# A four-layer hybrid network on one core: split down product with streamed weights, and a rearranged attention opening

## The reference, cut to what matters

```python
x = x + attn_a(layernorm(x))   # 16 heads of 16, rope, causal, LoRA on q, k, v, o
x = x + ffn(layernorm(x))      # 4 experts, the best one for each row
x = x + mamba(layernorm(x))    # chunked scan, gate, norm
x = x + ffn(layernorm(x))      # the same weights again

# ffn
probs = softmax(x @ Wr + br);  top_w, top_idx = top_k(probs, 1)
h = silu(x @ Wg[e]) * (x @ Wu[e])          # 256 -> 1024
y = (h @ Wd[e]) * top_w                    # 1024 -> 256, e = top_idx
```

## Time and profile before

| | us |
|---|---|
| median of 3 runs | 2194.78 |
| lowest and highest | 2182.81, 2199.73 |
| the profiled execution's own time | 2185.0 |
| its span, first to last instruction | 2183.1 |

### The profile page before, as it was taken

The page is one execution under the profiler, slowest core; times in us unless marked ns, Lnnn a source line. Parts: engine busy times, 40 slices in busy tenths (PEclk is TensorE's granted clock), DMA queues, the critical chain, the costliest instruction groups (busy, mean ns, idle before and its releaser), DMA issues. The chain is left out here.

```text
span 2183.1 us, 30159 instructions
## 1 busy us (share of the span) xinstructions
PE 1819.3 (83%) x9520; PEld 1212.1 (56%) x9520; DVE 1191.3 (55%) x2979; ACT 822.7 (38%) x1705; POOL 725.6 (33%) x922
## 2 busy tenths in 40 slices
PE   5368889889888864899999658989898938999997
PEld 3133334434433322788888535747484727888886
DVE  4466676666666508543443356665656685443442
ACT  2036655656665624111111035554646441111111
POOL 2335464464462312222222124333242312222221
PEclk9569989989988855999999969999999978999999
DMA  5522333332442108000000230100101080000000
GB/s 160 174 89 90 119 126 95 122 125 77 134 135 87 39 16 313 22 24 28 26 25 26 70 111 15 43 36 1 78 1 78 1 309 22 26 24 30 25 24 9
DMA packets 90179, 161.23 MB, mean 74 GB/s; under 512 B 23080, under 2 KB 50476, under 8 KB 88880
## 3 DMA queue, kind: packets, MB, share of 16 engines
q1 hardware_dynamic: 71504, 107.39, 14.7%
q0 software_dynamic: 17984, 50.62, 7.2%
q10 hardware_dynamic: 544, 1.31, 0.2%
HBM read 102.52 MB, written 45.48 MB: 68 GB/s over the span
## 5 line engine op out<-in xcount | busy, mean ns | idle before, releaser
L690 ACT ACTIVATE a_probs<-a_ps_e 128x512 f32<-128x512 f32 (+3 forms) x768 | 336.0, 491 | 204.1 <-PE a_ps_e L854 200.9
L438 DVE CUSTOM_DVE_ANT_0 a_ps_m<-a_ps_m,a_causal 128x512 f32<-128x512 f32 (+3 forms) x512 | 239.4, 517 | 97.5 <-PE a_ps_m L841 96.4
L1433 PE MATMUL g_ps_y<-g_w_d,x_res 128*128 x1120 | 253.2, 379 | 2.8 <-DVE x_res L1203 2.8
L854 PE MATMUL a_ps_e<-a_q_st,a_k_st 64*128 64x512 f32 (+3 forms) x768 | 187.9, 480 | 76.4 <-ACT a_probs L690 48.5
L854 PEld LDWEIGHTS a_ps_e<-a_q_st,a_k_st 64*128 64x128 f32 x768 | 79.6, 201 | 289.8 <-ACT a_probs L690 200.5
L1433 PEld LDWEIGHTS g_ps_y<-g_w_d,x_res 128*128 128x128 f32 x1120 | 212.3, 190 | 34.6 <-issue 3.2
L442 DVE TENSOR_REDUCE a_peak<-a_ps_m 128x1 f32<-128x512 f32 x256 | 164.8, 686 | 94.8 <-PE a_ps_m L841 94.1
L841 PE MATMUL a_ps_m<-a_k_st,a_q_st 64*128 64x512 f32 (+3 forms) x768 | 152.7, 399 | 68.8 <-DMA a_k_st<-a_scr_k 28.0
L1323 ACT COPY x_res<-g_ps_h 128x512 f32<-128x512 f32 x70 | 41.1, 587 | 439.2 <-PE g_ps_h L1441 439.2
L576 POOL TENSOR_SCALAR_AFFINE_SELECT a_probs<-a_probs 128x256 f32<-128x256 f32 x256 | 103.9, 408 | 284.1 <-ACT a_probs L690 283.8
L1170 DVE BATCH_NORM_STATS2 g_xe_stats<-x_res 128x6 f32<-128x256 f32 x70 | 29.9, 426 | 295.6 <-DMA x_res<-g_x_rows,g_token_i 295.6
(11 more groups left out here) (272 smaller groups left out, 3664.5 us busy)
## 6 DMA issues: line engine op xcount, KB each, us to landing
a_q_st<-a_scr_q POOLq DMA_DIRECT2D x32, 512.0 KB, 4.0
a_k_st<-a_scr_k POOLq DMA_DIRECT2D x32, 512.0 KB, 4.8
m_spread_acs<-m_acs_rows SPq DMA_DIRECT2D x8, 2048.0 KB, 9.7
a_scr_q<-a_high SPq DMA_DIRECT2D x36, 256.0 KB
a_scr_k<-a_high SPq DMA_DIRECT2D x36, 256.0 KB
a_swapped<-a_raw SPq DMA_DIRECT2D x64, 128.0 KB, 2.0
g_w_gu<-L_ffn_Wg SPq DMA_DIRECT2D x8, 1024.0 KB, 9.8
g_w_gu<-L_ffn_Wu SPq DMA_DIRECT2D x8, 1024.0 KB, 12.4
```

The costliest lines, as they stand in the source:

```text
L438: nc.vector.tensor_tensor_reduce(ps_m[:, bank, 0:w], ps_m[:, bank, 0:w], causal[:, 512 - w:], 1.0, MASKED, ALU.add, ALU.max, peak[:, p % 2 ...
L690: nc.scalar.activation(probs[:, N % RING, r, q0:], ps_e[:, (2 * N + r) % HEAD_BANKS, q0:], ACT.Exp, scale=DH ** -0.5).then_inc(exp_done, 1)
L854: nc.tensor.matmul(ps_e[:, (2 * N + r) % HEAD_BANKS, q0:], k_st[rows(r), p % BUFS, j * P:(j + 1) * P], q_st[rows(r), p % BUFS, 512 * c + q ...
L1433: last = nc.tensor.matmul(ps_y[:, 0:D], hid_t[:, f * P:(f + 1) * P], w_d[:, bass.ds(e, 1), f].rearrange("p a d -> p (a d)"), start=(f == 0 ...
```

## The change

Expert layers: `Wd` isn't kept in SBUF. During the last attention units it is split once into a high and a low float32r part and written to a DRAM tensor `down_rows` (`load_down` on SP, `round_down` on ACT, `lower_down` on POOL, `store_down` on SP). For each slot POOL gathers the 128 rows of its expert, 16 KB each, into one of two buffers (`stream`), by a row index that DVE makes from the owner of the slot. The hidden rows are split too: ACT copies both halves to `hid_hi`, DVE subtracts for `hid_lo`. The down product has 8 float32r products of 512 columns (high by high and low side by side) and 8 of 256 (low by high); the result takes two operations. On DVE `center` now comes first in a turn and `stats` last, on POOL `root` last.

Attention: q and k pieces stand at steps 2, 8, 14, 20, and so do the v pieces; swaps, rotations, roundings, remainders and keeps are moved to match, the last of them into the next unit (`ROPE_THEN`). Parts 2 and 3 of block 0 have buffers of their own for high and low (`parts`); ACT issues the keeps of its parts 1 and 3. `put_rows` goes from POOL to SP, and the rows are rounded by ACT's copy. The loads of x for batches 1 to 3 wait for the first pair of heads. The moments of batch 1 stand between maxima, those of batches 2 and 3 in units 1 and 5. The diff, cut to its core:

```diff
-    LORA_AT, XT_AT, OUT_AT, QK_AT, V_AT, LORA_O_AT = (1, 4, 9), (6, 7, 12, 13), (15, 17, 19, 21), (3, 5, 7, 9), (3, 5, 7, 9), 13
+    LORA_AT, XT_AT, OUT_AT, QK_AT, V_AT, LORA_O_AT = (1, 4, 9), (6, 7, 12, 13), (15, 17, 19, 21), (2, 8, 14, 20), (2, 8, 14, 20), 11
...
+        first_high = spare[:, 2560:3584].rearrange("p (n q) -> p n q", n=2)
+        first_low = spare[:, 3584:4608].rearrange("p (n q) -> p n q", n=2)
...
+        wd_raw = [w[:].rearrange("p i q -> p (i q)") for w in (raw, rope)]
+        wd_high = [[x_t[:, 0], x_t[:, 1]], [xn[:].rearrange("p t d -> p (t d)"), swapped[:].rearrange("p i q -> p (i q)")]]
+        wd_rows = C["wd_rows"].rearrange("(e p) (t a d) -> e p t a d", p=P, t=FF // P, a=2)
+        WD_AT = {12 * CORE + 10 + 14 * e: e for e in range(EXPERTS)}
...
+        def parts(blk, i):
+            if blk == 0 and i >= 2:
+                return first_high[:, i % 2], first_low[:, i % 2]
+            return high[:, i % 2], low[:, i % 2]
+
+        def keep(eng, blk, i):
+            eng.wait_ge(low_ready, 4 * blk + i + 1)
+            n, half = i % 2, i // 2
+            to = scr[n][blk % 2, :, :, :, half * 512:(half + 1) * 512]
+            hi, lo = parts(blk, i)
+            for c, part in enumerate(((hi, hi, None, lo), (hi, lo, None, hi))[n]):
+                if part is not None:
+                    eng.dma_start(to[:, c], part).then_inc(scr_out[i % 2], 16)
...
+            def put_rows(p):
+
+                sp.wait_ge(piece_act, ACT_NO["max", p] + 1)
+                for r in range(2):
+                    sp.dma_start(q_st[64 * r + 32:64 * r + 33, p % BUFS, :].bitcast(F32), less_t[r * T:(r + 1) * T, p % 2, :]).then_inc(rows_in[p % BUFS], 16)
...
+            def load_down(e):
+                sp.wait_ge(low_ready, 4 * 2 * BATCH)
+                if e >= 2:
+                    sp.wait_ge(wd_out, 48 * (e - 1))
+                sp.dma_start(wd_raw[e % 2].rearrange("p (t d) -> p t d", d=D), A["Wd"][e].rearrange("(t p) d -> p t d", p=P)
+                             ).then_inc(wd_in, 16)
+
+            def store_down(e):
+                sp.wait_ge(wd_less, 4 * (e + 1))
+                sp.dma_start(wd_rows[e, :, :, 1], wd_raw[e % 2].rearrange("p (t d) -> p t d", d=D)).then_inc(wd_out, 16)
+                for k in range(2):
+                    sp.dma_start(wd_rows[e, :, 4 * k:4 * k + 4, 0], wd_high[e % 2][k].rearrange("p (t d) -> p t d", d=D)
+                                 ).then_inc(wd_out, 16)
...
             for i in range(4):
                 swap(0, i)
-            for i in range(4):
-                keep(0, i)
+            for i in (0, 2):
+                keep(sp, 0, i)
+            sp.wait_ge(pair_in[0], 32)
             for b in range(1, BATCH):
                 sp.dma_start(X[:, b * T:(b + 1) * T], x[:, b * T:(b + 1) * T]).then_inc(x_in[b], 16)
-            for i in range(4):
+            for i in range(3):
                 swap(1, i)
-            for i in range(4):
-                keep(1, i)
+            keep(sp, 1, 0)
+            put_rows(0)
+            swap(1, 3)
+            for i in (1, 2):
+                keep(sp, 1, i)
+            put_rows(1)
+            keep(sp, 1, 3)
...
                 for n in range(CORE):
+                    for p in MAX_AT.get(U * CORE + n, []):
+                        put_rows(p)
...
-                    if g % 2 == 1 and more and n in (4, 6, 8, 11):
-                        swap(2 * b + 2 + g // 2, (4, 6, 8, 11).index(n))
-                    if g % 2 == 1 and more and n in (17, 19):
-                        keep(2 * b + 2 + g // 2, (17, 19).index(n))
-                    if g % 2 == 0 and U >= 2 and (U - 1) // GROUPS + 1 < BATCH and n in (3, 6):
-                        keep((U - 1) // GROUPS * 2 + 2 + (U - 1) % GROUPS // 2, 2 + (3, 6).index(n))
+                    if g % 2 == 1 and more and n in (3, 9, 15, 21):
+                        swap(2 * b + 2 + g // 2, (3, 9, 15, 21).index(n))
+                    if g % 2 == 1 and more and n in (14, 20):
+                        keep(sp, 2 * b + 2 + g // 2, (14, 20).index(n))
+                    if g % 2 == 0 and U >= 2 and (U - 1) // GROUPS + 1 < BATCH and n in (3, 9):
+                        keep(sp, (U - 1) // GROUPS * 2 + 2 + (U - 1) % GROUPS // 2, 2 + (3, 9).index(n))
                     if n == (22 if g == 0 else 11):
                         collect(U, 0)
+                    if U * CORE + n in WD_AT:
+                        load_down(WD_AT[U * CORE + n])
+                    if U * CORE + n - 21 in WD_AT:
+                        store_down(WD_AT[U * CORE + n - 21])
...
-            for b in range(1, BATCH):
-                dve.wait_ge(x_in[b], 16)
-                moments(b)
-            maxima(0, CUTS[0])
+            for k in range(0, CUTS[0], 2):
+                maxima(k, k + 2)
+                if k in range(22, 22 + 2 * T, 2):
+                    row_moments(1, (k - 22) // 2)
+                if k == 42:
+                    moments(1)
...
+                    if g == 1 and b + 2 < BATCH and n in range(10, 10 + T):
+                        row_moments(b + 2, n - 10)
+                    if g == 1 and b + 2 < BATCH and n == 20:
+                        moments(b + 2)
...
+            def lower_down(e, k):
+                pool.wait_ge(wd_rounded, 4 * e + k + 1)
+                part = wd_raw[e % 2][:, 512 * k:512 * k + 512]
+                high_part = wd_high[e % 2][k // 2][:, 512 * (k % 2):512 * (k % 2) + 512]
+                nc.gpsimd.tensor_tensor(part.bitcast(F32R), part, high_part, ALU.subtract).then_inc(wd_less, 1)
...
                 if i >= 1:
                     remainder(1, i - 1)
-                if i == 2:
-                    put_rows(0)
+            inverse_std(1)
             remainder(1, 3)
-            put_rows(1)
-
-            ROPE_AT = {6: (0, 0), 7: (0, 1), 8: (0, 2), 9: (1, 0), 10: (1, 1), 11: (1, 2), 12: (2, 0), 13: (2, 1),
-                       14: (2, 2), 15: (0, 3), 17: (1, 3), 19: (3, 0), 21: (3, 1), 23: (3, 2)}
+
+            ROPE_AT = {5: (0, 0), 6: (0, 1), 7: (0, 2), 11: (1, 0), 12: (0, 3), 13: (1, 1), 14: (1, 2), 17: (2, 0),
+                       18: (1, 3), 19: (2, 1), 20: (2, 2), 23: (3, 0)}
+            ROPE_THEN = {0: (3, 1), 1: (2, 3), 2: (3, 2), 7: (3, 3)}
...
+                    if g % 2 == 0 and U >= 2 and (U - 1) // GROUPS + 1 < BATCH and n in ROPE_THEN:
+                        blk, (i, part) = (U - 1) // GROUPS * 2 + 2 + (U - 1) % GROUPS // 2, ROPE_THEN[n]
+                        if part < 3:
+                            rotate(blk, i, part)
+                        else:
+                            remainder(blk, i)
+                    for k in range(4):
+                        if U * CORE + n - 11 - 2 * k in WD_AT:
+                            lower_down(WD_AT[U * CORE + n - 11 - 2 * k], k)
...
-                    for p in MAX_AT.get(U * CORE + n - 1, []):
-                        put_rows(p)
+                    if g == 1 and b + 2 < BATCH and n == 22:
+                        inverse_std(b + 2)
...
-                    nc.scalar.copy(less_t[:, k % 2], bank[0:2 * T, 0:P]).then_inc(piece_act, 1)
+                    nc.scalar.copy(less_t[:, k % 2].bitcast(F32R), bank[0:2 * T, 0:P]).then_inc(piece_act, 1)
...
-                if blk >= 1 or i >= 2:
+                if blk >= 1:
                     act.wait_ge(scr_out[i % 2], 48 * (2 * blk + i // 2))
-                nc.scalar.copy(high[:, i % 2].bitcast(F32R), raw[:, i]).then_inc(high_ready, 1)
+                nc.scalar.copy(parts(blk, i)[0].bitcast(F32R), raw[:, i]).then_inc(high_ready, 1)
...
                     for i in range(4):
                         round_high(0, i)
+                    for i in (1, 3):
+                        keep(act, 0, i)
                 if e in ACT_NO:
...
-                    if g % 2 == 1 and more and n in (11, 14, 21):
-                        round_high(2 * b + 2 + g // 2, (11, 14, 21).index(n))
-                    if g % 2 == 0 and U >= 2 and (U - 1) // GROUPS + 1 < BATCH and n == 2:
+                    if g % 2 == 1 and more and n in (10, 16, 23):
+                        round_high(2 * b + 2 + g // 2, (10, 16, 23).index(n))
+                    if g % 2 == 0 and U >= 2 and (U - 1) // GROUPS + 1 < BATCH and n == 5:
                         round_high((U - 1) // GROUPS * 2 + 2 + (U - 1) % GROUPS // 2, 3)
...
-        w_d = sb("w_d", [P, EXPERTS, FT, D])
+        with nc.sbuf_tensor(name + "later", [P, 4608 + P], F32) as held_later:
+            later = held_later[:]
+        w_d = sb("w_d", [P, 2, FT, 2 * D], F32R)
...
-        hid_t = flat[:, 0:FF]
-        rows = flat[:, FF:FF + 2 * D].rearrange("p (a d) -> p a d", a=2)
+        hid_hi, hid_lo = C["hid"]
+        row_index = sb("row_index", [P, SLOTS], U32)
+        rows = flat[:, 2 * FF:2 * FF + 2 * D].rearrange("p (a d) -> p a d", a=2)
...
-            sp.wait_ge(turned_ps, HALVES)
-            for e in range(EXPERTS):
```

(64 more changed lines are left out.)

54 lines of the change are left out of this document (28 added, 26 removed).

## The result

The changed kernel takes 2263.4 us in the median of four runs (2260.2 to 2265.8), the kernel before 2192.1 in the four runs beside it (2182.8 to 2199.7): a ratio of 1.032 (95% interval 1.028 to 1.036). It is slower by 71 us where I forecast +3. The profiled execution has a span of 2258.5 us for 2183.1.

The account below looks back on a forecast made before the run. PE bounds the expert slots, while attention shows waits on exponentials, the k tile and rows of maxima. Attention -33 and expert layers +36 sum to +3 on 2194.8, giving 2198 us; range 2120 to 2265, the forecast's own 2180 to 2218.

Parts of the forecast that it names:

- the expert slots: Both expert layers: a slot goes from 10.11 to 10.65 us, +35 us over some 66 slots (+3 to +115).
- The loop: Expert slots: result, send, fetch, stream, root, center, combine, hidden transposes close once a slot, about 9.55 us + S.
- S: Expert slots: POOL's issue of the stream gather with 16 KB rows, taken as 1.1 us (0.6 to 2.3).
- Rival A: Expert slots: the loop over POOL doesn't bind, PE alone sets 9.56 us a slot; 2127 us in all; chance 0.22.
- Rival B: Expert slots: S is 2 us or more, 66 us per us; 2258; against it, 0.60 for 4 KB rows; chance 0.23.
- only stalls between them can go, and PE's shown waits in the units are short: -3 (0 to -10): Attention units: spreading the same projections can only remove stalls, -3 us (0 to -10).
- the opening: Start of attention: first scores at 65.5 to 66, maxima no longer only at 88.45; -23 us (-10 to -26).
- The step by which the last writes are issued until about 54 and the loads go at about 59.6: Opening: own buffers and ACT's queue end write issue at about 54, not 60.74; loads follow 5.6 us later.
- rival C: Opening: writes on two queues land no sooner, x comes late, DVE waits for it amid maxima; +20, 2218; chance 0.11.
- the rows of maxima, -11, and in part -7: Attention: moving the rows from POOL's to SP's queue saves 7 us at the first unit, 11 in others (0 to -24).
- the split of the down weights, +6: Units 12 to 14: ACT's 9.9 us of roundings cost 6 (0 to 20); POOL's 20.6 us of subtractions hide.
- The loads of w_d that go were waited for by nothing: Expert layers: nothing on the chain waited for the removed w_d loads, so no gain was counted from dropping them.

Follow-up runs that it names:

- second run: Changed kernel with the steps of before for projections, swaps, roundings, rotations, remainders and writes in the attention units: 2223.2 us, ratio 1.013.
- third: Changed kernel with only POOL's fourth-part rotation moved from step 23 to steps 1 to 3 of the next unit: 2265.4 us.
- eighth: Changed kernel with POOL's rotations each one or two steps later behind their swaps, projections still spread: 2256.0 us, ratio 1.030.
- tenth run: Changed kernel with attention steps of before, expert turns reordered so nothing ahead of combine waits, and k's first-part write back on SP: 2165.3 us.
- seventh run: Second run with the rows of maxima back on POOL's queue: 2229.4 us, ratio 1.017.
- ninth run: Changed kernel with attention steps of before, DVE's stats after combine and center last, POOL's stream first, then root, send, fetch: 2137.6 us, ratio 0.974.

## Why the prediction was right or wrong

**Right: the expert slots.** Forecast 10.65 us and +35 us over the slots, measured 10.72 and +32. The loop has the operations and the gaps that I summed, S among them with 0.99 for 1.1. Rival A was wrong as an outcome of this order, and right as the floor under it: with the loop cut and the stream early the slot is 9.49, where I gave PE alone 9.56. Rival B's S did not come: rows of 16 KB cost POOL what rows of 1 KB do, 1.00 in the mean of 70 streams; its price of 66 us for every us of S no run tested. Its counter-argument read only the cheaper of two equal loads: the earlier trace rows show 0.80 and 0.60 for rows of 4 KB. The rule of the Trainium skill that I weighed ("DMA: Bandwidth & Descriptors", section "Anatomy of one DMA — SWDGE (gpsimd) path"), by which many descriptors can be emitted before their number adds to the cost, is not contradicted by this 1.00; no view here shows whether the longer rows took more descriptors at all.

**Wrong: "only stalls between them can go, and PE's shown waits in the units are short: -3 (0 to -10)".** This step failed, and it carries the miss. The second run shows 40 us for the spread projections and what moves with them. I looked at PE's waits in the kernel before, which such a move could remove, and not at what POOL has to do behind each projection: rotation of three operations, which waits for SP's swap, and remainder, in the same queue as the masks. I should have asked what the moved work stands in front of on POOL: the fourth part's rotation went from steps 19 to 23 into steps 23 to 2, the first masks of the next unit. My bounds held no loss at all, for which no reason stood in the text. And I had no term for the clock: the short units of before (1, 5, 9 and 11) run at 1.00 throughout, and the windows of the change show 0.50 for some 10 us behind such a wait. By the windows of the second run half of the 40 us is slower products and half waiting, most of that for masks. Of what makes masks and exponentials late, the third and eighth runs show that POOL's waits at the swaps are the smaller part (0 and 7 us came back, 13 at most). How the rest divides between POOL's operations among the masks, ACT's copies amid the exponentials and the place of PE's projections is left open.

**Wrong in size: the opening.** The step by which the last writes are issued until about 54 and the loads go at about 59.6 failed: 61.12 and 67.26. The fourth part's rotation, which I had put at its old time (49.77), ends only at 51.52, ACT issues nothing for k until the fourth part is rounded (51.56), and the writes don't get quicker by a second queue: by the windows the DMA engines moved 151 to 198 GB/s from 48 to 64 us in the change and 158 to 190 before. The tenth run started the write 3.8 us sooner and gained nothing, which speaks for the rate. The k tile after its issue was as forecast: from the end of the first pair's issue to the scores 4.0 us, 4.8 expected, where it was 7.7. Of the 15.0 us by which the maxima start sooner, 2.8 are earlier scores (3.7 from the loads, less 0.9 from the later release), and 12.2 are the moments that no longer stand ahead of the maxima; part of these comes back between them, and 12.3 are left at the first exponential. Of rival C the first half came true, writes on two queues that land no sooner, and the second didn't: no wait of DVE for x is in the changed trace's attention.

**Wrong: the rows of maxima, -11, and in part -7.** The waits went, most of the time didn't: unit 0 is 7.4 us shorter in the change, of which the seventh run gives 1 to 6 us to the rows, and in the others it gives nothing. I had counted a wait on PE as time of the unit, but what PE needed next, the mask from POOL, came ready no sooner: where the seventh run waits 1.9 to 3.1 us for the rows at the starts of units 2, 6 and 10, the second waits 2.9 to 3.1 us for the mask. This is the same error as in the opening, one step further on: I did not ask what is late next.

**Nearly right: the split of the down weights, +6.** Units 13 and 14 are 7.4 us longer in the change, 11.6 in the second run, where their clock is 0.77; the bounds were 0 and 20. The seventh run has 12.7 there with the rows on POOL, so the rows aren't the cause; that it is the split is by exclusion, it was not taken out by itself.

**Not in the sum.** The end of each expert layer costs 4 to 7 us more. The tail of the change:

```profile
2228.71 1.02 POOL L1324 DMA_INDIRECT g_w_d<-down_rows,g_row_index  x1 [0.30 <-issue]
...
2236.61 1.03 POOL L1331 DMA_INDIRECT out<-x_res,g_token_i  x1 [6.88 <-DVE x_res L1280]
2237.24 2.98 PE L1525 MATMUL g_ps_y<-g_w_d,hidden_high 128*128 128x512 f32 x8 [4.32 <-DMA g_w_d<-down_rows,g_row_index]
2240.01 1.85 PE L1530 MATMUL g_ps_y<-g_w_d,hidden_less 128*128 128x256 f32 x8
```

The last down product has no up product in front of it to cover its weights, which land 8.5 us after the start of their issue; it then takes 4.6 us, from 2237.24 to 2241.9, at a granted clock of 0.64, where it takes 2.96 in the slots at 1.00. "The loads of w_d that go were waited for by nothing" was true, but the streams in their place are waited for. That wait is a small part, though: in the ninth run, where no weights are waited for, the end takes 31.4 us, because the product then waits for the result in front of it and runs 5.5 us at 0.50; 2.9 of the 7.1 us are GpSimd's last DRAIN instruction (8.63 us for 5.78). The mamba stage, +7.5 us, needs no cause in the change: its code is the same in all runs, and it took 484.3 to 494.8 us in the fourteen profiled executions (484.8 in the seventh run, which has all of the change in the expert layers).

The total lay inside the range of 2120 to 2265, 2 us from its upper end and outside the forecast's own 2180 to 2218, for a reason that was in none of the cases: loop as forecast, attention 60 us off. The upper end had been set for a stream that costs POOL 2.1 us, so it is luck that the range held.

## What to carry to other kernels

Before moving work between engines' turns, list for each engine what stands behind every instruction that the moved one brings along, and give "it only smooths" a loss as its other bound: here the smoothing cost 40 us. In a loop over several engines, order the turns so that nothing ahead of the operation that PE needs next waits for anything issued after the last result; the same instructions took some 11.0, 10.72, 9.9 or 9.49 us a slot by their order alone. A transfer that must be there early is issued first, as soon as its buffer is free.

## What the runs showed of the hardware

- An indirect load of 128 rows of 16 KB takes GpSimd 1.00 us, one of 1 KB rows 1.02 in steady state: the time of the issue did not grow with the bytes of a row. Only transfers of 128 rows were made. Its 2.1 MB arrive in time for one slot every 9.49 us.
- Float32r products with 128 rows: eight of 512 columns and eight of 256 took 1.87 + 1.09 us at clock 1.00, 0.14 for a short one where a long one takes 0.23.
- In a wait of PE of 4.72 us the granted clock fell from 1.00 to 0.50, and it stayed there for some 10 us after work had resumed, with PE busy throughout 219 to 222 us.
- Scratch writes of 256 KB kept to 151 to 198 GB/s on one queue or two, while from 64 us on the kernel before moved 341 to 390, loads and x together.
- The DRAIN instruction that ends GpSimd's program of an expert layer took 8.63 us in both layers of the changed kernel and 5.77 and 5.78 us in the kernel before, which has 35 indirect transfers fewer in each layer. That these are the reason is not shown.
